# One transformer layer on one core: a first batch in another order, a factored transform of W2, and the first transposed scores ahead of the last down products

## The reference

```python
x = x + layernorm(attention(layernorm(x)))   # 16 heads of 16, rope on q and k, causal softmax, biases
x = x + layernorm(ffn(layernorm(x)))
# attention: qkv = x @ w_qkv.T + b_qkv; q, k = rope(q), rope(k)
#            out = softmax(q k.T / 4 + causal) v; return out @ w_out.T + b_out
# ffn:       hidden = fwht(silu(x @ W1.T) * (x @ W3.T)); return hidden @ W2.T
# fwht: Walsh-Hadamard transform over 1024 columns, scaled by 1/32
```

## Time and profile before

| | us |
|---|---|
| median of 3 runs (499.99 to 500.64) | 500.08 |
| profiled execution | 497.78 |
| its span | 496.1 |
| PE busy | 405.0 (82%) |
| PE weight loads busy | 338.2 (68%) |
| DVE busy | 281.2 (57%) |
| ACT busy | 210.9 (43%) |
| POOL busy | 162.1 (33%) |

### The profile page before, as it was taken

The page is one execution under the profiler, slowest core; times in us unless marked ns, Lnnn a source line. Parts: engine busy times, 40 slices in busy tenths (PEclk is TensorE's granted clock), DMA queues, the critical chain, the costliest instruction groups (busy, mean ns, idle before and its releaser), DMA issues.

```text
span 496.1 us, 7892 instructions
## 1 busy us (share of the span) xinstructions
PE 405.0 (82%) x2884; PEld 338.2 (68%) x2884; DVE 281.2 (57%) x936; ACT 210.9 (43%) x314; POOL 162.1 (33%) x284
## 2 busy tenths in 40 slices
PE   1679677999599997988599988987799979858992
PEld 1569645558489985557499975566699965448991
DVE  7554583625937776536856776267576754273114
ACT  4445234753323337843423347813332367423221
POOL 4136002533512226514422235614132245321232
PEclk9999865999969999999889999999799999997998
DMA  6549900000397000200695001102880002000001
GB/s 230 215 136 247 212 1 1 2 2 0 127 255 171 1 1 1 85 1 1 179 245 130 1 1 42 44 1 72 219 201 21 1 1 85 1 1 1 1 1 42
DMA packets 35463, 36.95 MB, mean 74 GB/s; under 512 B 2016, under 2 KB 34528, under 8 KB 35424
## 3 DMA queue, kind: packets, MB, share of 16 engines
q1 hardware_dynamic: 35424, 36.45, 26.6%
HBM read 21.76 MB, written 14.68 MB: 73 GB/s over the span
## 4 chain that ended last, share of the span: by engine, by line
PE 58%; DVE 13%; DMA 9%; issue 7%; ACT 6%; SPq 3%; POOL 2%; DVEq 0%; POOLq 0%; ACTq 0%
PE ps L266 30%; PE ps L448 8%; PE ps L464 7%; PE ps L436 5%; DMA qk_scratch<-qk_s 4%; DMA q_t<-qk_scratch 4%; ACT probs L656 4%; DVE masked_scores L923 2%; SPq L293 2%; DMA raw_bias<-in_b_out 2%; PE ps L498 2%; DVE xy L985 1%; POOL hid_s L803 1%; PE ps L405 1%; DVE stats_h L870 1%
## 5 line engine op out<-in xcount | busy, mean ns | idle before, releaser
L923 DVE CUSTOM_DVE_ANT_0 masked_scores<-ps,mask_row 128x128 bf16<-128x128 f32 (+3 forms) x256 | 114.4, 488 | 61.6 <-PE ps L436 61.1
L266 PE MATMUL ps<-xt,w_s 128*128 128x256 f32 x768 | 111.7, 294 | 0.0
L266 PEld LDWEIGHTS ps<-xt,w_s 128*128 128x128 f32 x768 | 106.2, 202 | 0.5
L803 POOL TENSOR_TENSOR hid_s<-gate,hid_s 128x512 fp32r<-128x512 f32 x32 | 41.2, 1287 | 135.9 <-ACT hid_s L668 135.9
L656 ACT ACTIVATE probs<-ps 128x1280 f32<-128x1280 f32 x64 | 76.4, 1242 | 9.5 <-PE ps L448 8.9
L436 PE MATMUL ps<-k_t,q_t 96*128 96x128 f32 (+3 forms) x256 | 71.7, 356 | 9.8 <-DMA q_t<-qk_scratch 5.6
L448 PEld LDWEIGHTS ps<-q_t,k_t 128*128 128x128 f32 x256 | 44.9, 198 | 32.2 <-ACT probs L656 14.7
L266 PE MATMUL ps<-w_s,hid_s 128*128 128x256 f32 x384 | 55.5, 284 | 7.0 <-POOL hid_s L803 7.0
L448 PE MATMUL ps<-q_t,k_t 128*128 128x512 f32 (+3 forms) x256 | 55.7, 345 | 5.6 <-ACT probs L656 4.0
L266 PEld LDWEIGHTS ps<-w_s,hid_s 128*128 128x128 f32 x384 | 51.6, 190 | 9.3 <-POOL hid_s L803 8.7
L436 PEld LDWEIGHTS ps<-k_t,q_t 96*128 96x128 f32 x256 | 43.0, 198 | 18.6 <-DVE maxima L923 10.9
(11 more groups left out here) (99 smaller groups left out, 485.3 us busy)
## 6 DMA issues: line engine op xcount, KB each, us to landing
qk_scratch<-qk_s SPq DMA_DIRECT2D x32, 256.0 KB, 5.6
k_t<-qk_scratch SPq DMA_DIRECT2D x16, 384.0 KB, 5.5
q_t<-qk_scratch SPq DMA_DIRECT2D x8, 768.0 KB, 8.8
qk_scratch<-qk_s SPq DMA_DIRECT2D x8, 512.0 KB, 5.5
xa<-in_x SPq DMA_DIRECT2D x4, 512.0 KB, 9.6
xy<-in_x SPq DMA_DIRECT2D x4, 512.0 KB, 3.5
out<-xy SPq DMA_DIRECT2D x8, 256.0 KB, 2.3
o_t<-in_w SPq DMA_DIRECT2D x1, 1024.0 KB, 10.0
```

The source lines that it names most:

```text
L266: ins = eng.matmul(o, lhs(i), rhs(j), start=first and n == 0, stop=last and n == 2, skip_group_check=skip)
L803: pool.tensor_tensor(hid_s[:, a % 2, 1, :], gate[:, a % 2, :], hid_s[:, a % 2, 0, :].bitcast(F32), ALU.subtract).then_inc(S["hid_l"], 1)
L923: ins = dve.tensor_tensor_reduce(masked_scores[:, SCORE_NO[n] % 2, i * keys:(i + 1) * keys], ps[:, banks[n], i * keys:(i + 1) * keys], mas ...
```

## The change

- Prologue: x is loaded first. Fourteen products of zeros (k_t by k_t, into bank 7) run before the first turns. The low part of w_qkv is made behind `norm_x`, half by VectorE and half by POOL. The bias copies stand behind those of x on ACT; `sixty_fourth` is made by POOL. Products for queries and keys (`q`) and for values (`b`) are apart, and the values come behind. A tile's product waits for that tile's xt_l alone. POOL's rope product has two buffers.
- The second half's stores wait until the first half is fetched (`qk_in`), in batch 0.
- The transform of W2 is factored: POOL makes three levels of butterflies between the eight row groups, then TensorE one level of 128, with 16 products for 128.
- The low parts of wo, w3, w1 and the transformed W2 are made by VectorE: wo after the mix, W2, w3 and w1 in batch 0's attention. The load of xr for batch 0 waits for w3's.
- In attention: the tails move one head earlier (3, 4, 5), the last turn one later (8), and ACT's and POOL's part for them stand after heads 6 and 8.
- The down products of step 7 move from the end of feed_forward to behind the scores of head 1 of the next attention (not in the last batch). `UNITS_AFTER` puts all 42 pieces ahead of them. The load of the exponential's table moves from behind `hid_high` of step 7 to behind its `silu`.
- VectorE makes the next x's statistics ahead of batch 0's tails.

```diff
 TAIL_BANKS = [6 + n % 2 for n in range(TAIL)] + [7]
-TAIL_AFTER = {4: (0, 2), 5: (2, 4), 6: (4, 6), 7: (6, 7)}
+TAIL_AFTER = {3: (0, 2), 4: (2, 4), 5: (4, 6), 8: (6, 7)}
...
-MIX = """o0 o1 d0 d1 n0 n1 q0 l0 l1 e0 c0 o2 d2 y0 o3 s0 n2 y1 l2 d3 s1 n3 y2 v0 l3 q1 r0 y3 s2 s3 e1 c1 t0
-    v1 e2 c2 q2 R0 r1 R1 w0 R2 R3 t1 q3 w1 r2 e3 c3 N0 N1 N2 t2 r3 N3 t3 H0 L0 H1 L1 H2 L2 H3 L3 u0 u1
+MIX = """o0 o1 d0 d1 n0 n1 q0 b0 l0 l1 e0 c0 o2 d2 y0 o3 s0 n2 y1 l2 d3 s1 n3 y2 v0 l3 q1 b1 r0 y3 s2 s3 e1 c1 t0
+    v1 e2 c2 q2 b2 R0 r1 R1 w0 R2 R3 t1 q3 b3 w1 r2 e3 c3 N0 N1 N2 t2 r3 N3 t3 H0 L0 H1 L1 H2 L2 H3 L3 u0 u1
     u2 u3""".split()
...
 UNIT_BANKS = unit_banks(EARLY_UNITS)
 FIRST_UNIT_BANKS = [4 + n % 4 for n in range(N_UNITS - 1)] + [5] + TAIL_BANKS
 PROBS = 10
-FIRST_SELECTOR = [None, 0, 2, 9]
-FIRST_TRANSFORM = [-1, -1, -1, -1, -1, 4, 8, 13]
-FIRST_W2_PARTS = [14, 19]
+FIRST_SELECTOR = {2: 0, 3: 2}
+BUTTERFLIES_BEFORE = [0, 4, 13]
+FIRST_W2_PARTS = {"split": 18, "transform": 33, "words": 36, "high": 38}
 ROOT_AFTER = 5
 
...
                     fetch_q(0)
+                    if b == 0:
+                        sp.wait_ge(S["qk_in"], 48)
...
             sp.dma_start(sel[QK_ROWS:P, :], selector).then_inc(S["selector_in"], 16)
-            load_x(0)
             sp.dma_start(raw_wqkv.rearrange("p (c n) -> p c n", c=CH),
...
             load_xr(0)
             pack_qk(1, EARLY_SEND[1])
...
 
+                pe.wait_ge(S["xt_l"], b * TILES + t + 1)
+                if t >= 2:
+                    pe.wait_ge(S["qk_copied"], b * TILES + t - 1)
+                lhs = lambda c: (lambda s: xt[:, s, c, t * P:t * P + P])
+                for c in range(CH):
+                    triple(pe, ps[:, t % 2, :], lhs(c), lambda s: wqkv_s[:, s, c, 0:2 * DIM], c == 0, False)
+                if b == 0 and t == 0:
+                    pe.wait_ge(S["sixty_made"], 1)
+                    pe.wait_ge(S["bias_s"], 1)
+                    pe.wait_ge(S["bias_l"], 1)
+                pe.matmul(ps[:, t % 2, :], sixty_fourth[:, :], bias_s[:, 0:2 * DIM], start=False, stop=True)\
+                  .then_inc(S["qk_done"], 1)
...
+
+            def values_product(b, t):
+
+                lhs = lambda c: (lambda s: xt[:, s, c, t * P:t * P + P])
                 if t == 0:
                     pe.wait_ge(S["xt_l"], b * TILES + TILES)
                 else:
-                    if t >= 2:
-                        pe.wait_ge(S["qk_copied"], b * TILES + t - 1)
...
                 pe.wait_ge(S["maxed"], (b + 1) * N_SCORES - TAIL)
+                pe.wait_ge(S["hidden"], b * HCH)
                 for h in range(HEADS + PV_LAG):
...
                         score_t(b, h)
+                    if h == DOWN_AFTER and b:
+                        for t in range(TILES):
+                            down(b - 1, HCH - 1, t)
...
+                    elif kind == "down" and (n < HCH - 1 or b == BATCHES - 1):
                         down(b, n, i)
                     elif kind == "unit":
...
+                                        w2_s[:, part, c, :], start=(c % 2 == 0 and part == 0),
+                                        stop=(c % 2 == 1 and part == 1), skip_group_check=True)
                 ins.then_inc(S["transformed"], 1)
 
+            pe.wait_ge(S["zeroed"], 2)
+            for n in range(14):
+                pe.matmul(bank(7), k_t[0:QK_ROWS, 0, 0:P], k_t[0:QK_ROWS, 1, :], start=True, stop=True, skip_group_check=True)
             pe.wait_ge(S["eye_in"], 16)
             for t in range(TILES):
                 turn_x(0, t)
-            pe.wait_ge(S["split_l"], 1)
-            pe.wait_ge(S["bias_h"], 2)
-            pe.wait_ge(S["bias_l"], 1)
+            pe.wait_ge(S["wqkv_l"], 2)
             mix(-1, FIRST_MIX)
...
             for n in range(N_UNITS):
                 score_unit(0, n, FIRST_UNIT_BANKS)
-                for c in range(HCH):
-                    if FIRST_TRANSFORM[c] == n:
-                        transform(c)
+                if n == FIRST_W2_PARTS["transform"]:
+                    pe.wait_ge(S["v_copied"], TILES)
+                    transform()
...
             for b in range(BATCHES - 1):
                 attend(b, True)
+                if b == 0:
+                    pe.wait_ge(S["wo_l"], 1)
+                    pe.wait_ge(S["out_bias"], 2)
+                    pe.wait_ge(S["w1_l"], 1)
+                    pe.wait_ge(S["w3_l"], 1)
+                    pe.wait_ge(S["transformed_l"], 1)
...
                         silu(b, n)
+                        if n == HCH - 1:
+                            act.activation(spare[:, :], minus_half[:, 0:1], ACT.Exp)
                     elif kind == "gate":
                         hid_high(b, n)
...
             select(0)
+            select(1)
             act.wait_ge(S["w_qkv_in"], 16)
             split(wqkv_s, raw_wqkv)
-            act.wait_ge(S["bias_in"], 32)
-            act.activation(bias_h, raw_bias, ACT.Copy).then_inc(S["bias_h"], 1)
-            act.activation(bias_s[0:P // 2, :], raw_bias[0:P // 2, :], ACT.Copy)
-            act.wait_ge(S["eye_in"], 16)
...
-            act.activation(w2_s[:, 0, :, :].rearrange("p c n -> p (c n)"), raw_w2, ACT.Copy).then_inc(S["w2_h"], 1)
+            act.wait_ge(S["bias_in"], 32)
+            act.activation(bias_h[:, 0:3 * DIM], raw_bias[:, 0:3 * DIM], ACT.Copy).then_inc(S["bias_h"], 1)
+            act.activation(bias_s[0:P // 2, 0:3 * DIM], raw_bias[0:P // 2, 0:3 * DIM], ACT.Copy).then_inc(S["bias_s"], 1)
             mix(-1, FIRST_MIX)
...
-                                   ps[:, 0:4, :].rearrange("p a n -> p (a n)"), ACT.Copy, scale=W2_SCALE)\
+                for part, unit in FIRST_SELECTOR.items():
+                    if unit == n:
+                        select(part)
+                if n == FIRST_W2_PARTS["split"]:
+                    act.wait_ge(S["w2_turned"], 3)
+                    act.activation(w2_s[:, 0, :, :].rearrange("p c n -> p (c n)"), mixed_w2, ACT.Copy).then_inc(S["w2_h"], 1)
+                if n == FIRST_W2_PARTS["words"]:
+                    act.wait_ge(S["transformed"], 1)
+                    act.activation(raw_w2, ps[:, 0:4, :].rearrange("p a n -> p (a n)"), ACT.Copy, scale=W2_SCALE)\
+                       .then_inc(S["transformed_words"], 1)
+                if n == FIRST_W2_PARTS["high"]:
+                    act.wait_ge(S["transformed_words"], 1)
...
-                if t >= 1:
-                    pool.wait_ge(S["rotated"], b * TILES + t)
-                o = rot_s.rearrange("p (h e i) -> p h e i", e=2, i=HALF)
+                if t >= 2:
+                    pool.wait_ge(S["rotated"], b * TILES + t - 1)
+                o = (rot_s, rot_s_odd)[t % 2].rearrange("p (h e i) -> p h e i", e=2, i=HALF)
...
-                    for n in range(*TAIL_AFTER.get(h + 1, (0, 0))):
-                        max_low(b, TAIL_UNITS[n])
+                    if h in TAIL_COPY_AFTER:
+                        max_low(b, TAIL_UNITS[TAIL_COPY_AFTER[h]])
                     if h == ROOT_AFTER and order is MIX:
                         root(b + 1, "x")
...
+                    pool.wait_ge(S["w2_turned"], n)
+                a, o = (w.rearrange("p (u e n) -> p u e n", e=2, n=DIM << n) for w in (src, dst))
+                pool.tensor_tensor(o[:, :, 0, :], a[:, :, 0, :], a[:, :, 1, :], ALU.add)
+                pool.tensor_tensor(o[:, :, 1, :], a[:, :, 0, :], a[:, :, 1, :], ALU.subtract).then_inc(S["w2_turned"], 1)
...
-            for n, (w, raw) in enumerate(((wo_s, raw_wo), (w3_s, raw_w3))):
-                pool.wait_ge(S["split_h"], n + 3)
-                pool.tensor_tensor(w[:, 1, :, :].rearrange("p c n -> p (c n)"), raw,
-                                   w[:, 0, :, :].rearrange("p c n -> p (c n)").bitcast(F32), ALU.subtract)\
-                    .then_inc(S["split_l"], 1)
             for n in range(N_UNITS):
+                if n in BUTTERFLIES_BEFORE:
+                    butterflies(BUTTERFLIES_BEFORE.index(n))
                 max_low(0, n)
+                if n in (FIRST_W2_PARTS["split"], FIRST_W2_PARTS["split"] + 2):
+                    w2_low((n - FIRST_W2_PARTS["split"]) // 2)
...
+                if order is MIX:
+                    layer_x(b + 1)
                 if b == 0:
+                    split(w2_s, raw_w2, "transformed_h", 1, "transformed_l")
                     for n in TAIL_UNITS:
                         score_unit(b, n, FIRST_UNIT_BANKS)
-                if order is MIX:
-                    layer_x(b + 1)
+                    split(w3_s, raw_w3, "split_h", 4, "w3_l")
+                    dve.wait_ge(S["transformed_l"], 1)
                 copy_o(b, 0)
                 if order is MIX:
                     norm_x(b + 1)
+                if b == 0:
+                    split(w1_s, raw_w1, "split_h", 3, "w1_l")
```

137 lines of the change are left out of this document (69 added, 68 removed).

## The result

The changed kernel is slower, by 1.8%. The median of four runs is 508.93 us (507.24 to 511.19), that of the kernel before, beside it, 500.03; the ratio is 1.0181, with a 95% interval of 1.0138 to 1.0225. The forecast was 494.3, with 489 to 498.5 as its range: wrong in sign. The profiled execution of the changed kernel took 511.19 us.

The account below looks back on a forecast made before the run. The prologue's chain up to the first transposed score at 80.36 and three batch boundaries were taken to bound the kernel. Prologue -8.4, batch 0's attention -0.8, boundaries 0, turn's waits +3.4 sum to -5.8: 494.3 us, range 489 to 498.5.

Parts of the forecast that it names:

- It waits 1.7, and behind it stand all further value products: Boundaries into batches 1 and 2: TensorE waits 1.7 for the last tail unit's low part on POOL; 3.4 lost.
- Rival (c): Boundaries: the new waits lower the granted clock, costing 1.56 each, 4.7 for three, so 499.0; chance 0.09.
- In batch 0 the statistics are done early: Batch 0's attention: with the next x's statistics made early, the 1.7 wait for the turn does not arise there.
- the same rule that the prediction used in the prologue: POOL: a VectorE operation of two SBUF inputs holds POOL for its length.
- The two balance: the first value products stay: Three boundaries: earlier scores offset later norm_z, value products stay at 199.0 to 199.2; gain 0, bounds -0.5 to +1 each.
- The prologue: 2.6 of 8.4: Prologue: first transposed score at 72.0 and not 80.36, 8.4 gained.
- The first store: Prologue: first store to scratch at 22.6, 6.9 earlier than 29.53.
- The serial transfers: Prologue: late stores wait for the early fetch; late fetch landed at 53.4, so 5.8 left of 6.9.
- Rival (b): Prologue: both fetches take 10.0 and contend with the x load; late fetch at 56.5, time 497.4; chance 0.14.
- the stall of VectorE: Prologue's late stage: VectorE runs out of work behind the transformed W2's low parts; 2.7 lost, stage 18.6.
- three signs of being wrong: Turn's wait missing, POOL's 1024-wide operations well over 2.3, or the early fetch not the gate of the late stores.
- The rival with the long time: Prologue, rival (d): butterflies take 5.9 each, not 2.31; first transposed score at 90.7, time 513; chance 0.05.

Follow-up runs that it names:

- Down_back: Changed kernel with POOL's root of x behind the last tail maxima's low part, down products and table load back as before: 496.36 us, ratio 0.9945.
- units_back: Changed kernel with POOL's root of x behind the last tail maxima's low part, and `UNITS_AFTER` as before: 505.62 us, ratio 1.0142.
- start_only: Changed kernel with boundaries, tails, turn, pieces and table load as before; prologue and batch 0's statistics and splits stay changed: 495.80 us, ratio 0.9944.
- Experiment 11: start_only without the `qk_in` wait, tails one head earlier, turn at head 7, and POOL's w_qkv half behind `norm_x`: 487.30 us, ratio 0.9768.
- experiments 1 and 9: 1 is start_only, ratio 0.9944; 9 is start_only without the `qk_in` wait ahead of the second stores: 492.03 us, ratio 0.9874.

## Why the prediction was wrong

**The turn's wait: place and length right, its price not.** The step "It waits 1.7, and behind it stand all further value products" in batches 1 and 2 was met by 1.75 and 1.78, released by POOL's max_s, and no wait came in batch 3. But each cost 3.5 from values to turn, since the clock fell behind it. The sum has the wait alone, 3.4 for both. Rival (c) did name the clock behind the two new waits, at a chance of 0.09, and priced it by the start of an attention stage: 499.0, still 10 below what was measured. What a fall costs is shown by the turns of several runs: without it a wait of 1.46 cost 1.7 and one of 2.02 cost 2.1; with it waits of 1.75 to 2.03 cost 3.4 to 5.1. Whether it comes is not settled by the length of the wait, and no run here shows what settles it. Taking the three waits away gave 6.4 by the ratios, of which they are 5.0; the 1.4 over them are within the noise of the medians, and it is the traces that show the clock's part.

**"In batch 0 the statistics are done early"** was true and not enough. The w3 split, costed at nothing since it lies in VectorE's idle time, held a cut on POOL until it ended, by the same rule that the prediction used in the prologue. The step failed by leaving out what else a free VectorE's operation touches.

**"The two balance: the first value products stay", "Gain 0".** From the last silu to the values the boundary nearly balanced: 15.68 to 15.92 for 15.45. But the last silu itself comes later (1.3, 2.1 and 0.9), with two more pieces ahead of it, a term that the prediction doesn't have at all. With these pieces gone from behind the last up products, the values should have come the sooner, and they did not. Down_back shows what the down products took of it: its last silu is as late (1.7, 2.3 and 0.5 more than before), but the values follow after 13.96, 14.74 and 13.96. Behind two heads' scores the down products make norm_z late, TensorE waits 2.75 for it, and what follows runs in part at the low clock. Their place and that of the table load cost 5.4. My bound of +1 a boundary was too narrow and set against the wrong stretch. Nor had the pieces filled a large stall before: the wait for the hidden part is 1.49 with two more pieces behind the last up products, and 1.76 in down_back without them.

**The prologue: 2.6 of 8.4.** That is the profiled execution; the profiles of runs with this prologue and its wait have the first transposed score at 76.3 to 78.1, so 2.3 to 4.1 were gained. Three terms were off.

(1) The first store, at 25.23 and not 22.6. Of this 0.8 is the clock: in eight of the ten profiles whose code is the same up to there, the first six products took 1.60 to 1.63 and the first store fell at 24.4 to 24.5, while in the changed kernel's and in units_back's they took 2.78 and 2.86, at a granted clock of 0.70 and then 0.50, and the store fell at 25.2 and 25.4. Most of the rest is the order on VectorE: in start_only the sine products of tile 1 ended at 20.63, as forecast (20.6), but their sum, forecast at once, started at 22.04, behind the cosine product of tile 2 and a low part of tile 0 (read from the trace; no run tried another order). And I had POOL delayed by VectorE at the w_qkv split and never VectorE by POOL: norm_x took 2.90 for 1.38. The Trainium skill, GPSIMD Engine Reference, section "Specifications", names contention also with VectorE's instructions in a 2-port mode, where I had used only the half on two SBUF inputs; no run here shows the mode in which norm_x runs. Experiment 11 shows the hold, and that it is worth only half a us.

(2) The serial transfers. From the first store to the landing of the late fetch it took 29.7 before; 30.8 were forecast for the change, and it took 32.5. In start_only it is 32.1, and without the wait on `qk_in` 29.3. So the wait's price was 2.8 in the traces and 3.5 by the ratios of experiments 1 and 9, where the forecast had 1.1. Rival (b) at 0.14 had the place, but not by fetches at 10.0: they took 8.82 and 8.98.

(3) In the late stage the stall of VectorE was 3.23 (2.7 forecast), and ACT's two operations on the transformed W2 (1.88 and 1.91) stood ahead of the last high part of the maxima, which I had not counted; it came about 0.5 late by them. A butterfly took 2.34 to 2.52, near the forecast from the split alone. What the factored transform by itself gives I did not try.

None of the three signs of being wrong that the prediction gave came true: the wait at the turn was there, the butterflies took 2.3 to 2.5, and the early fetch was the gate of the late stores. They tested whether the steps are there and not what they cost.

The rival with the long time was the wrong one: butterflies at 5.9 each.
